# Writing out the loops inside an image in a four-layer convolution kernel

## The chip, the cores and the metric

One core of one Trainium2 chip runs the whole program. The metric is device time in microseconds, the median of several executions. The engines are TensorE (PE for its matmuls, PEld for its weight loads), VectorE (DVE), ScalarE (ACT), GpSimd (POOL) and SyncE (SP), which issues most of the DMAs.

## The reference, cut to what matters

The input is x of 4 x 32 x 256 x 256 floats (image, channel, row, column). Four layers follow each other, each with a group normalisation (16 groups) ahead and a residual around it:

```python
x = x + L0(gn(x))   # 3x3 convolution on values quantised to int8
x = x + L1(gn(x))   # DFT over rows and columns, a 32x32 channel mix at 2 x 32 x 32 modes, inverse DFT
x = x + L2(gn(x))   # 1x1 convolution, then a 5x5 depthwise convolution with filters pooled from its own output
x = x + L3(gn(x))   # per position: weights from maxima of 3x3 patches, relu, times the patch, mean of 9 taps
```

L0's scale needs the largest value of the whole input, so all of x is read once ahead of the images.

## The kernel before, in words

**Layout.** An image lies in on-chip memory as 128 partitions, one for each of 32 channels and each parity of row and column, with 128 x 128 pixels in the free dimension, padded to 130 x 130 (`img`). A tile is 4 rows of 128 pixels, 512 columns; there are `NT` = 32 tiles in an image, 16 pairs of tiles (`NPAIR`), and 16 blocks of 8 rows (`NBLK`).

**Order.** Every engine has its own program, written by hand, and they meet through counting semaphores: an instruction waits until a semaphore has reached a value. The loop over the four images is a Python loop in every engine's program, so it is written out. Inside an image some loops are Python loops too, and others are hardware loops (`Fori`): their body is stored once and runs with the loop variable in a register. In such a body a wait's value, as `b * (9 * NT) + j * 36 + (m + 13)`, and an address, as `ds(e * CR + ...)`, are worked out by register instructions of the engine's sequencer. SyncE's program has no such loop.

**Stages of an image**, with the lines that the change touches:

- Convolution L0: TensorE loops over 8 groups of 4 tiles (line 411, matmuls of line 420, nine a tile, each with a register address). ScalarE and VectorE feed and drain it, written out.
- L1: transposes (line 432, written out) that ScalarE (loop of line 625, copy of line 628) and VectorE (loop of line 1065, copy of line 1068) copy out; DFT matmuls (lines 446, 462); the mode mixing, in which GpSimd (loop of line 855, product of line 859) and VectorE (loop of line 1083, product of line 1088, sum of line 1092) work through 16 pieces of weights that SyncE loads; inverse DFT (lines 469, 481, 491); VectorE adds the result to the image and sums windows for L2 (loop of line 1127, lines 1117 and 1122).
- L2: TensorE (loop of line 504, matmuls of line 518, 36 for each block of 8 rows), GpSimd (loop of line 876, line 869), ScalarE (loop of line 701) and VectorE (loop of line 1240).
- L3's maxima: transposes (line 529), maxima on VectorE (loop of line 1259, line 1262).
- L3: the last and longest stage, described next.

**The last stage** goes through 32 tiles in pairs; two pairs are one pass of a loop on TensorE (line 575), ScalarE (line 806), GpSimd (line 880) and VectorE (line 1326). Some first or last passes are written out today: TensorE's first, VectorE's first and last, and half of ScalarE's last (`step(NT // 4 - 1, 0)`, line 809). For a tile TensorE forms nine products of five matmuls each (`product`, line 549), so 90 matmuls a pair. VectorE takes each product out of PSUM, with relu and times the patch (line 1298), into one of six buffers `pd_t`; it adds two of them up itself at three places of a pair (lines 1303 and 1307), and GpSimd adds the others one by one into the tile's sum `acc_t` (line 895; 15 adds a pair, each waiting for the one before). ScalarE prepares features of the next pair: copies into PSUM (`shifted`, lines 737 and 738), after which VectorE takes maxima (`front`, lines 1271, 1274) and subtracts (1277), and ScalarE casts (745) and copies sides (757 to 765). Between these, in ScalarE's own order, stand `restore` (line 770) and `store`:

```python
def store(j, v):
    act.wait_ge(s_acc, b * NADDS + j * (2 * ADDS) + (v // 2 * ADDS + pool_adds(v % 2, 8) + 8))
    act.dma_start(out[b, :, ds(j * (4 * TILE) + v * TILE, TILE)], acc_t[v % 4]).then_inc(s_out[v % 4], 16)
```

The store waits for GpSimd's last add of its tile, and whatever follows it in ScalarE's program, the next pair's `shifted` among it, is queued behind it. VectorE's program of a pair (`pair`, line 1279) puts `front`'s first step after its fifth product (m == 4), so its sixth waits for ScalarE's copies; TensorE may be 6 products ahead of VectorE (wait of line 560). GpSimd's fourth add in a pair's second tile waits for VectorE's sum of line 1303 (wait of line 891). SyncE loads each pair's rows from DRAM one to two pairs ahead (lines 337 to 346).

Of the kernel before, what the change touches and what calls it, by code (L numbers as in the profile page):

```python
# [82 lines left out]
def build(nc, x, w0, b0, w2, w2t, b2, mixw, w3a, w3b, bn, cst, out):  # L83
    with ExitStack() as ctx:
# [304 lines left out]
        def _(pe):  # L389
# [19 lines left out]
            for b in range(B):  # L409

                with pe.Fori(0, NCH) as e:
                    for v in range(4):
                        if v == 0:
                            pe.wait_ge(s_q, b * (NCH + 1) + e + 1)
                        if v == 3:
                            pe.wait_ge(s_q, b * (NCH + 1) + e + 2)

                        pe.wait_ge(s_t0, b * NT + e * 4 + (v + 1))
                        for s in range(9):
                            mm = T.matmul(bank(v), taps0[:, P * s:P * s + P],  # L420
                                          qgrid[:, ds(e * CR + (v * RT + s // 3), RT), s % 3:s % 3 + WO],
                                          start=(s == 0), stop=(s == 8))
                        mm.then_inc(s_conv0, 1)
# [79 lines left out]

                with pe.Fori(0, NBLK // 2) as j:
                    for p in range(2):
# [67 lines left out]
                for v in range(1, 4):  # L573
                    tile(0, v)
                with pe.Fori(1, NT // 4) as j:
                    for v in range(4):
                        tile(j, v)
# [3 lines left out]
        def _(act):  # L581
# [21 lines left out]
            for b in range(B):  # L603
# [20 lines left out]

                with act.Fori(0, NT // 4) as j:
                    for k in range(2):
                        act.wait_ge(s_l1pe, b * L1PE + j * 4 + (2 * k + 1))
                        A.copy(xt.rearrange("p (m r) -> p m r", r=HO)[:, :, ds(j * (4 * RT) + 2 * RT * k, RT)],
                               psum[:, 2 + 2 * k, :].rearrange("p (r m) -> p m r", r=RT)).then_inc(s_l1act, 1)
# [70 lines left out]
                copy_third(0, 1)  # L700
                with act.Fori(1, NBLK // 2 - 1) as j:
                    high2(j, 1)
                    sums(j - 1, 1)
                    copy_third(j, 0)
                    high2(j + 1, 0)
                    sums(j, 0)
                    copy_third(j, 1)
# [97 lines left out]

                with act.Fori(0, NT // 4 - 1) as j:
                    step(j, 0)
# [5 lines left out]
        def _(pool):  # L813
# [38 lines left out]
            for b in range(B):  # L852

                hold(pool, s_spec, b + 1)
                with pool.Fori(0, 2) as j:
                    for k in range(8):
# [18 lines left out]
                hold(pool, s_x2, b * NT + NT)  # L875
                with pool.Fori(1, NBLK // 2) as j:
                    for p in range(2):
                        transform(j, p)

                with pool.Fori(0, NT // 4) as j:  # L880
                    for v in range(4):
# [21 lines left out]
        def _(v):  # L903
# [93 lines left out]
            for b in range(B):  # L997
# [66 lines left out]

                with v.Fori(0, NT // 4) as j:
                    for k in range(2):
# [15 lines left out]
                hold(v, s_spec, b + 1)  # L1082
                with v.Fori(0, 2) as j:
                    pooled = [k for k in range(8) if k not in WR_DVE]
# [40 lines left out]
                for k in range(8):  # L1125
                    add_wave(0, k)
                with v.Fori(1, NT // 8) as j:
                    for k in range(8):
# [110 lines left out]
                add_conv2(0, 1)  # L1239
                with v.Fori(1, NBLK // 2 - 1) as j:  # L1240
                    low2(j, 1)
# [16 lines left out]
                mx_rq = mxt.rearrange("p (q r) -> p r q", q=4)  # L1258
                with v.Fori(0, NT // 4) as j:
                    for k in range(4):  # L1260
# [64 lines left out]
                pair(0, 1)  # L1325
                with v.Fori(1, NPAIR // 2 - 1) as j:
                    pair(j, 0)
# [105 lines left out]
```

## Time and profile before

| what | value |
|---|---|
| median of 3 executions | 3294.06 us (3288.66 to 3294.98) |
| the profiled execution | 3293.31 us |
| its span, first to last instruction | 3291.5 us |
| mean granted TensorE clock | 0.935 of full speed |
| instructions in the span | 45789 |
| TensorE busy | 2702.1 us (82%) |
| VectorE busy | 2660.9 us (81%) |
| GpSimd busy | 1831.8 us (56%) |
| ScalarE busy | 1813.8 us (55%) |

Register, branch and semaphore instructions, and those that issue a DMA, are counted as instructions but not as busy time. The busy shares are over the whole span; a stage can have another limit than the span's busiest engine. The profile's chain of work is followed back from the last instruction, at each step to what released it; "issue" in it is time in which the engine waited for nothing that the profile shows, and an engine's name with a q (ACTq, POOLq) is its sequencer: a register instruction, a wait, a branch or the issue of a DMA.

### The profile page before, as it was taken

The numbers are of one execution on the slowest core, as the hardware profiler recorded it, in microseconds if no ns is written. First come the engines' busy times: TensorE is split into PE (matmuls) and PEld (weight loads), VectorE is DVE, ScalarE is ACT, GpSimd is POOL, SyncE is SP. The second block draws the span as 40 slices with busy tenths as digits, with TensorE's granted clock in tenths as the row PEclk, the third lists the DMA queues.
The fourth block names the chain that finished last, engine by engine and source line by source line (L and its number), as shares of the span: only waits on it lengthen the run. The fifth ranks groups of instructions, "written<-read, shape, count | busy, mean of one in ns | idle before, by whom it ended". The sixth has DMA issues, their size and how long they took to land. (4 is left out here: it accounts for less than half of the span.)

```text
span 3291.5 us, 45789 instructions
## 1 busy us (share of the span) xinstructions
PE 2702.1 (82%) x12733; PEld 2092.2 (64%) x12733; DVE 2660.9 (81%) x3579; ACT 1813.8 (55%) x2343; POOL 1831.8 (56%) x1296
## 2 busy tenths in 40 slices
PE   0086698899989579799999569889998957979998
PEld 0035577677757458577774468667775745857776
DVE  8985887788885898688888598878888499868887
ACT  7743655566543455565655265566564345555654
POOL 2013173599950436199990317269995044629998
PEclk9998899999999789899999879999999978989999
DMA  6732001988860200688880200289885020068984
GB/s 254 251 91 77 1 0 38 231 220 222 193 174 1 77 1 0 169 222 218 209 228 32 77 0 0 56 230 225 218 192 158 1 77 0 0 183 218 227 208 114
DMA packets 116200, 419.22 MB, mean 127 GB/s; under 512 B 16565, under 2 KB 30693, under 8 KB 105354
## 3 DMA queue, kind: packets, MB, share of 16 engines
q1 hardware_dynamic: 96058, 374.65, 44.1%
q10 hardware_dynamic: 18432, 38.54, 3.3%
q0 software_dynamic: 1616, 4.90, 0.5%
q8 instruction: 44, 0.72, 0.1%
q14 instruction: 50, 0.41, 0.0%
HBM read 340.57 MB, written 75.26 MB: 126 GB/s over the span
## 5 line engine op out<-in xcount | busy, mean ns | idle before, releaser
L895 POOL TENSOR_TENSOR work<-work 128x512 f32<-128x512 f32 x960 | 1283.3, 1342 | 415.4 <-DVE work L1307 314.8
L549 PE MATMUL psum<-workr,w 128*128 128x512 f32 (+1 forms) x5760 | 1366.9, 397 | 67.2 <-ACT workr L765 50.6
L549 PEld LDWEIGHTS psum<-workr,w 128*128 128x128 f32 (+1 forms) x5760 | 1086.5, 189 | 346.9 <-issue 51.4
L1298 DVE SCALAR_TENSOR_TENSOR work<-psum,work 128x512 f32<-128x512 f32 x1152 | 738.1, 679 | 34.9 <-POOL work L895 21.4
L518 PE MATMUL psum<-workr 128*128 128x512 f32 x2304 | 553.7, 403 | 21.5 <-DVE workr L1195 21.5
L869 POOL TENSOR_TENSOR work<-img 128x520 f32 (+1 forms) x256 | 387.2, 1544 | 284.7 <-DVE workr L1167 255.7
L518 PEld LDWEIGHTS psum<-workr 128*128 128x128 f32 x2304 | 441.6, 192 | 135.0 <-issue 24.7
L859 POOL TENSOR_TENSOR work<-work 128x1024 f32<-128x1024 f32 x40 | 114.1, 2886 | 485.2 <-DVE work L1081 483.0
L745 ACT CAST workr<-psum 128x650 fp32r<-128x650 f32 x128 | 90.0, 703 | 419.4 <-DVE psum L1274 411.8
L420 PE MATMUL psum<-work,taps 128*128 x1152 | 261.6, 391 | 44.4 <-DVE work L1039 44.4
L1271 DVE TENSOR_TENSOR psum<-psum,work 128x650 f32<-128x650 f32 x128 | 107.9, 843 | 210.0 <-ACT psum L738 209.7
L420 PEld LDWEIGHTS psum<-work,taps 128*128 128x128 bf16 x1152 | 114.2, 99 | 191.2 <-issue 59.7
L668 ACT ACTIVATE workr<-work 128x1040 fp32r<-128x1040 f32 x128 | 136.5, 1073 | 76.9 <-PE psum L518 76.8
L620 ACT ACTIVATE work<-psum,small 128x512 f32<-128x512 f32 x128 | 99.3, 776 | 120.2 <-PE psum L420 94.3
L757 ACT CAST workr<-workr 32x512 fp32r<-32x512 f32 x256 | 158.8, 620 | 7.2
L758 ACT CAST workr<-workr 32x512 fp32r<-32x512 f32 x256 | 158.2, 618 | 6.2
L684 ACT ACTIVATE work<-img 128x1024 f32 (+1 forms) x64 | 68.0, 1063 | 161.5 <-DVE img L1233 161.5
L1307 DVE TENSOR_TENSOR work<-work 128x512 f32<-128x512 f32 x128 | 150.3, 1174 | 0.0
L1216 DVE SCALAR_TENSOR_TENSOR work<-psum,small,work 128x512 f32<-128x512 f32 x128 | 90.2, 747 | 57.2 <-ACT work L676 57.1
L737 ACT COPY psum<-work 64x650 f32<-64x650 f32 x128 | 89.5, 699 | 85.1 <-POOL work L895 61.0
L491 PE MATMUL psum<-consts,work 128*128 128x128 f32 x1024 | 123.8, 278 | 13.7 <-DVE img L1117 7.0
L642 ACT COPY work<-psum 64x512 f32<-64x512 f32 x64 | 57.9, 1060 | 139.9 <-PE psum L481 139.9
(188 smaller groups left out, 3582.6 us busy)
## 6 DMA issues: line engine op xcount, KB each, us to landing
work<-gn_dram SPq DMA_DIRECT2D x256, 585.0 KB, 10.7
work<-gn_dram SPq DMA_DIRECT2D x256, 146.2 KB, 3.8
work<-gn_dram SPq DMA_DIRECT2D x128, 292.5 KB, 4.8
work<-in_x SPq DMA_DIRECT2D x16, 2048.0 KB, 7.2
img<-in_x SPq DMA_DIRECT2D x32, 1024.0 KB, 11.4
work<-in_mixw SPq DMA_DIRECT2D x64, 512.0 KB, 4.9
out_x<-work ACTq DMA_DIRECT2D x120, 256.0 KB, 6.4
gn_dram<-img SPq DMA_DIRECT2D x24, 1040.0 KB, 16.9
```

What stands on the lines that cost most here:

```text
L420: mm = T.matmul(bank(v), taps0[:, P * s:P * s + P], qgrid[:, ds(e * CR + (v * RT + s // 3), RT), s % 3:s % 3 + WO], start=(s == 0), stop=( ...
L491: mm = T.matmul(bank(2 + g % 4)[:, P * r:P * r + P], gsp[:, RT * g + r, :], cs("idftw"), start=True, stop=True)
L518: mm = T.matmul(bank(banks[p]), wt[:, at:at + P], urow(part, i)[:, :, dx:dx + WO], start=(dx + n == 0), stop=(dx + n == 4))
L549: mm = T.matmul(bank(m % 6), w5[wt][0:kr, P * n:P * n + P], ft[0:kr], start=(i == 0), stop=(i == 4))
L668: A.activation(uh[p][:, half], ut[p][:, half], ACT.Identity, scale=(0.5 if h == 0 else 1.0)).then_inc(s_uh, 1)
L757: A.copy(tile4(dst[0:32, :]), left).then_inc(s_shh, 1)
L758: A.copy(tile4(dst[32:64, :]), up).then_inc(s_shh, 1)
L859: G.tensor_tensor(wr[k], wr[k], spec, ALU.mult).then_inc(s_prod, 1)
L869: G.tensor_tensor(urow(ut[p], i), x0, x1, op).then_inc(s_u, 1)
L895: G.tensor_tensor(acc_t[v], acc_t[v], pd_t[(9 * v + n) % 6], ALU.add).then_inc(s_acc, 1)
L1298: V.scalar_tensor_tensor(out=tile4(pd_t[m % 6]), in0=tile4(psum[:, m % 6, :]), scalar=0.0, in1=rv[:, q, y0:y0 + RT, x0:x0 + WO], op0=ALU.m ...
L1307: V.tensor_tensor(two, pd_t[(9 * k) % 6], two, ALU.add).then_inc(s_two, 1)
```

## The change

All fifteen hardware loops become Python loops over the same ranges; nothing else is edited. Bodies, order, buffers and semaphores stay; every wait value and address is then a constant in the instruction. The diff, cut to its lines:

```diff
-                with pe.Fori(0, NCH) as e:
+                for e in range(0, NCH):
...
-                with pe.Fori(0, NBLK // 2) as j:
+                for j in range(0, NBLK // 2):
...
-                with pe.Fori(1, NT // 4) as j:
+                for j in range(1, NT // 4):
...
-                with act.Fori(0, NT // 4) as j:
+                for j in range(0, NT // 4):
...
-                with act.Fori(1, NBLK // 2 - 1) as j:
+                for j in range(1, NBLK // 2 - 1):
...
-                with act.Fori(0, NT // 4 - 1) as j:
+                for j in range(0, NT // 4 - 1):
...
-                with pool.Fori(0, 2) as j:
+                for j in range(0, 2):
...
-                with pool.Fori(1, NBLK // 2) as j:
+                for j in range(1, NBLK // 2):
...
-                with pool.Fori(0, NT // 4) as j:
+                for j in range(0, NT // 4):
...
-                with v.Fori(0, NT // 4) as j:
+                for j in range(0, NT // 4):
...
-                with v.Fori(0, 2) as j:
+                for j in range(0, 2):
...
-                with v.Fori(1, NT // 8) as j:
+                for j in range(1, NT // 8):
...
-                with v.Fori(1, NBLK // 2 - 1) as j:
+                for j in range(1, NBLK // 2 - 1):
...
-                with v.Fori(0, NT // 4) as j:
+                for j in range(0, NT // 4):
...
-                with v.Fori(1, NPAIR // 2 - 1) as j:
+                for j in range(1, NPAIR // 2 - 1):
```

## Rows read from the trace of the kernel before

**Rows 1.** The page: span, and busy time, share and instructions of two engines.

```profile
span 3291.5 us, 45789 instructions
...
PE 2702.1 (82%) x12733; PEld 2092.2 (64%) x12733; DVE 2660.9 (81%) x3579; ACT 1813.8 (55%) x2343; POOL 1831.8 (56%) x1296
```

**Rows 2.** Stages of image 2: length, busy PE PEld DVE ACT POOL, clock, DMA.

```profile
1191.70:1330.30 138.60, 138.47 (x576) 110.44 (x576) 116.62 (x120) 71.19 (x104) 85.45 (x54) 0.98 0.00 0
...
1375.30:1721.20 345.90, 341.66 (x1440) 271.62 (x1440) 290.66 (x425) 205.36 (x310) 310.74 (x234) 0.99 0.88 218
```

**Rows 3.** TensorE's timeline, last stage: start, length, line, count, idle before.

```profile
1432.75 42.59 PE L549 MATMUL psum<-workr,w 128*128 128x512 f32 x180 [0.61 <-DVE work L1298]
1475.96 42.58 PE L549 MATMUL psum<-workr,w 128*128 128x512 f32 x180 [0.62 <-DVE work L1298]
```

**Rows 4.** Busy time of line 549 alone: PE, PEld, clock, DMA, early stage.

```profile
1379.00:1431.50 52.50, 52.50 (x226) 42.23 (x225) 1.00 0.90 212
```

**Rows 5.** Chain that ended last, two pairs of image 4: start, length, what.

```profile
3053.91 9.62 PE psum L549 x40
...
3063.56 0.96 DVE work L1303
...
3064.68 0.08 POOL work L895
...
3070.15 1.64 POOL work L895
...
3072.31 0.04 ACTq L806
...
3072.69 0.04 ACTq L735
...
3072.77 0.07 ACT psum L737
...
3075.71 9.62 PE psum L549 x40
...
3085.36 0.76 DVE work L1303
...
3091.75 1.64 POOL work L895
...
3094.17 0.08 ACT psum L737
...
3097.12 0.97 PE psum L549 x3
```

**Rows 6.** ScalarE's timeline: the store in the written-out end of image 2.

```profile
1709.68 0.35 ACTq L775 DMA_DIRECT2D out_x<-work  x1
```

**Rows 7.** GpSimd's timeline, last stage: one pair's adds.

```profile
1637.70 20.91 POOL L895 TENSOR_TENSOR work<-work 128x512 f32<-128x512 f32 x15 [0.71 <-DVE work L1303]
```

**Rows 8.** VectorE's timeline around the start of the mode mixing.

```profile
1076.80 1.04 DVE L1079 TENSOR_TENSOR work<-psum,work 128x512 f32<-128x512 f32 x1 [2.37 <-PE psum L462]
1077.87 0.19 DVE L1081 TENSOR_TENSOR work<-work 128x32 f32<-128x32 f32 x1
1078.39 1.23 DVE L1088 TENSOR_TENSOR work<-work 128x1024 f32<-128x1024 f32 x1 [0.33 <-DVE work L1081]
1079.77 1.22 DVE L1092 TENSOR_REDUCE work<-work 128x1024 f32 x1 [0.16 <-DVE work L1088]
```

**Rows 9.** Line 420 alone at full clock (as rows 4); timeline of line 446.

```profile
970.00:1018.00 48.00, 48.00 (x223) 21.43 (x222) 1.00 0.00 0
...
1818.16 28.77 PE L446 MATMUL psum<-consts,work 128*128 128x64 f32 x256 [0.98 <-DVE work L1068]
```

**Rows 10.** DMA view: instruction queues, and a small load with median us to landing.

```profile
q8 instruction: 44, 0.72, 0.1%
q14 instruction: 50, 0.41, 0.0%
...
work<-gn_dram SPq DMA_DIRECT2D x256, 146.2 KB, 3.8
```

## The prediction

> **What bounds the kernel now.** I read the page first: TensorE is busy for 82% of the span and GpSimd for 56% [rows 1], but these are averages over stages with different limits. A table by stage for the second image, which is one of four alike and 778 us long, gives each its limit [rows 2]. The last stage (line 549) takes 345.9 of the 778 us, with TensorE busy for 341.7, GpSimd for 310.7 and the DMA engines at 88%. The convolution of line 518 takes 138.6 us and TensorE is busy for 138.5: registers can cost nothing there unless they slow the matmuls themselves.
>
> So I looked at TensorE's timeline in the last stage [rows 3]. It runs 180 matmuls in one piece of 42.6 us, idles 0.61 or 0.62 us for VectorE's line 1298, and does so again: the period is 1475.96 - 1432.75 = 43.21 us. An undisturbed stretch gives the floor [rows 4]: 226 matmuls touched in 52.50 us, the two outer ones cut, so 52.5/225 = 0.2333 us each and 180 x 0.2333 = 42.0 us. TensorE thus loses 1.2 us in every 180 matmuls (two "pairs" of output tiles; 90 each, floor 21.0 us).
>
> The chain of waits says who takes it [rows 5]. It is a ring that goes round once per pair: TensorE's eight products (9.62 us), VectorE's add of line 1303, five GpSimd adds of line 895, then ScalarE, which can start the next pair's copies (lines 737, 738) only after it has issued the store of line 775, which waits for the last of those adds; then VectorE, and TensorE's twelfth product. In this execution the ring takes 3075.71 - 3053.91 = 21.80 us where ScalarE turns its loop around (pair A) and 3097.12 - 3075.71 = 21.41 us where it doesn't (pair B). Together 43.21 us, as in image 2; both are above TensorE's 21.0.
>
> **What the change does, part by part.** It writes out fifteen loops on four engines: three on TensorE, ScalarE and GpSimd each, six on VectorE. SyncE's program has no such loop and stays as it is, so no load is queued differently. Removed are register arithmetic ahead of waits and addresses, and branches. The waits stay, with constants; where an instruction has two, one becomes a wait instruction of its own (the parts written out today show this form).
>
> *ScalarE in the ring.* From the end of GpSimd's add to the start of line 737 takes, in pair A, from 3070.15 + 1.64 = 3071.79 to 3072.77, 0.98 us; in pair B from 3091.75 + 1.64 = 3093.39 to 3094.17, 0.78 us [rows 5]. In between lie two register instructions, the store's issue (a DMA instruction), in A the branch of line 806 (3072.31 to 3072.69), and register work for the waits of lines 734 and 735. The written-out form of the store stands at an image's end: its issue takes 0.35 us [rows 6]. With hops of up to 0.04 us, as between lines 735 and 737 in the chain (3072.73 to 3072.77), I make the new path 0.03 + 0.35 + 0.04 + 0.02 + 0.04 = 0.48 us. A saves 0.50, B 0.30.
>
> The branch in it costs 3072.69 - 3072.31 = 0.38 us with its register work [rows 5]. The Trainium skill (Advanced Engine Details and Errata, Control Flow Timing) puts a compare-and-branch at about 108 ns. By that figure A would save about 0.23 instead of 0.50, and the stage's gain would be 28 x 0.27 = 7.6 us smaller; the chain row has the branch in place, so the sum goes by the row.
>
> *GpSimd in the ring.* From VectorE's end (3063.56 + 0.96 = 3064.52) to the add's start (3064.68) it takes 0.16 us, with two register instructions in it. A wait instruction and the add must stay; I take 0.06 us saved, bounds 0 and 0.12 (nothing left but the 0.04 us hops). Between adds nothing but the previous add's end is waited for, and the next one's register instructions run in that time: nothing saved, bounds -0.02 to 0.02 us each.
>
> *VectorE and TensorE in the ring.* VectorE's register instructions run under its own 0.7 us operations, TensorE's under matmuls: nothing. Their cover, the queue ahead of a busy engine, stays.
>
> Sum for the stage: A saves 0.50 + 0.06 = 0.56 of the 0.80 us that it lies above TensorE's floor, B 0.30 + 0.06 = 0.36 of 0.41. What is late next is TensorE's own pace, 0.24 and 0.05 us behind. Together 0.92 us, seven times an image (the first of the eight double passes starts with nothing late), four images: 28 x 0.92 = 25.8 us. GpSimd comes close behind as the next limit: its 15 adds of a pair take 20.91 us and then it idles 0.71 us [rows 7]; 20.91 + 0.10 = 21.0 us, level with TensorE.
>
> *The mode mixing (lines 1083 to 1092).* VectorE works nearly without a pause here. Where one of its operations waits for the one before through a register, the idle time is 0.16 us; with a constant it is 1077.87 - (1076.80 + 1.04) = 0.03 us [rows 8]. Six such places an image, one of them hidden under a wait for GpSimd: 5 x 0.11 = 0.5 us, four images 2.0 us (bounds 0 and 0.7 an image).
>
> *Loop entries* on VectorE (lines 1065, 1083, 1127, 1259): entering that of line 1083 left 0.33 us idle, 0.3 more than a wait with a constant [rows 8]. The other three follow other work and wait for TensorE anyway, so I count one: 0.3 us an image, 1.2 us in all (bounds 0 and 2).
>
> *First convolution (line 420).* Every matmul has a register address there. At full clock they come at 48.00/222 = 0.216 us [rows 9], while 512 columns at 2.4 GHz take 0.213. I take 0; the bound is 288 x 0.003 = 0.9 us an image. The other TensorE loops have constant addresses.
>
> *Instruction supply.* Written-out code is fetched once and longer. Today the two instruction queues bring 44 + 50 packets [rows 10]. 12733 matmuls run, 3183 an image [rows 1], of which by the code some 1346 belong to written-out text or the first pass of a loop, so packets should grow about 3183/1346 = 2.4 times, some 130 more. The written-out line 446 ran 256 matmuls in 28.77 us, 0.112 us each, without a gap [rows 9], faster than any loop would use up text, and line 549's first 180 matmuls, written out, ran at the same 0.2333 us as the loop. I take 0; what it costs if the cover fails is a rival.
>
> Total: 25.8 + 2.0 + 1.2 = 29.0 us. The profiled execution took 3293.31 us (span 3291.5), 0.75 us under the median, so 3264.3 us by it and **3265.1 us** against the median of 3294.06.
>
> **The rivals.**
> *Only part of the ring gets shorter* (0.14). The register work runs ahead of the event it waits for, and the branch's time is mostly that of the wait behind it. Then A saves some 0.2 and B 0.1 us: 28 x 0.3 = 8.4 us, with 1.6 us elsewhere 3284. For it: on VectorE the same instructions cost nothing. Against: in the chain each stands after the add's end.
>
> *TensorE's floor is reached everywhere* (0.14). Then 1.21 us per two pairs go, 28 x 1.21 = 34 us, with 3 us from mixing and entries 3257. It needs 0.24 us more in pair A and 0.05 in B than I count; for it speaks that the first pairs, where nothing is late yet, run at the floor, so a slack once there is used up slowly.
>
> *The place goes to GpSimd* (0.06). The last of the five adds takes 1.64 us, the four before it (3070.15 - 3064.68)/4 = 1.37 us with the hop to the next [rows 5]; perhaps it meets a VectorE operation. If in the new phase two of the five do, some 0.3 us come back per pair, and if line 1303 takes pair A's 0.96 us in B too (0.76 now), 0.20 per two: 56 x 0.3 + 28 x 0.20 = 22 us, leaving 7: 3287.5 us and above, within 0.2%.
>
> *Instruction supply stalls, slower* (0.06). The place is ScalarE, VectorE and GpSimd in the last stage, whose text grows most and whose fetches share DMA engines that are 88% busy [rows 2]. The nearest price is a small load there, 3.8 us from issue to landing [rows 10]. Some 130 more packets; if 20 of them fall on the ring uncovered, 20 x 3.8 = 76 us less 29: 3341 us. It decides from 29/3.8 = 8 uncovered fetches. Against it: the first, written-out pairs of that stage show no such hole.
>
> The Trainium skill (Runtime: NRT & Kernel Launch, Instruction fetch mechanics) says that the sequencer fetches ahead in order and that crossing a block is mostly hidden, but that the buffer has only two blocks on most engines. The first half agrees with line 446; whether two blocks suffice under loaded DMA no trace here shows.
>
> That the change does nothing is excluded: the register instructions are part of the span's 45789 [rows 1] and must go.
>
> **How the numbers follow.** The forecast has 0.60. Low end: all of TensorE's idle time (34), 0.7 x 4 for mixing, 2 for entries, 1 of line 420's 3.6: 40 us, 3254. High end: the partial case, 3284, which leaves out the GpSimd and fetch cases (0.12) and some of the edge. About 0.2% (6.6 us) is what a measurement of this kernel tells from no change. Faster by more: 0.60 + 0.14 + 0.14 = 0.88; within: 0.06; slower: 0.06.
>
> **What would show it.** The page should count several thousand instructions fewer; TensorE's timeline in the last stage should have its period fall from 43.2 to 42.3 us with one gap left per two pairs; the chain should go from line 895 to line 737 in about 0.5 us; VectorE's gaps in the mixing should be 0.03 us; lines 518 and 420 should stand. GpSimd's idle time per pair should fall from 0.71 to some 0.2 us. Gaps ended by nothing that the profile shows, with an instruction packet just before their end, would make it wrong, and so would a period of 43 us with the register instructions gone.

## The result, and the profile after

The changed kernel takes **3326.39 us** (median of 5 runs, 3323.82 to 3327.32) against 3290.32 us for the kernel before in the same comparison (5 runs, 3288.46 to 3294.98): ratio 1.0105, 95% interval 1.0091 to 1.0119. It is 36 us slower where 3265.1 us were forecast; the range ended at 3284.

The page of the changed kernel, its span and busy times, and the two instruction queues:

```profile
span 3324.6 us, 37611 instructions
...
PE 2699.3 (81%) x12733; PEld 2091.0 (63%) x12733; DVE 2634.0 (79%) x3579; ACT 1813.4 (55%) x2343; POOL 1865.4 (56%) x1296
...
q8 instruction: 101, 1.65, 0.2%
q14 instruction: 91, 0.75, 0.1%
```

There are 8178 instructions fewer than in [rows 1] (register work and branches gone, some wait instructions new), and the span is 33.1 us longer. The same two stages as in [rows 2], image 2 of the changed kernel (length, busy PE, PEld, DVE, ACT, POOL, clock, DMA):

```profile
1198.80:1336.40 137.60, 136.99 (x576) 109.39 (x576) 120.70 (x121) 70.81 (x104) 87.88 (x54) 0.99 0.00 1
1380.00:1736.30 356.30, 342.32 (x1440) 272.06 (x1440) 279.95 (x424) 206.50 (x312) 315.19 (x233) 0.99 0.86 213
```

These windows are not cut alike at both ends. From the first matmul to the end of the last, the convolution is 1.5 us shorter (138.47 and 136.99 us, TensorE busy throughout), and the last stage 9.5 us longer (345.9 and 355.3 us). Counted from the first image's first matmul, between the first matmuls of successive stages, the last stage with what follows it grows from 1427.5 to 1470.8 us in four images (+43.3), and everything else shrinks from 1687.4 to 1677.8 us (-9.7); together +33.6, where the span shows +33.1. So the question is one stage.

TensorE's timeline there, changed kernel (to be held against [rows 3]):

```profile
1439.84 21.30 PE L549 MATMUL psum<-workr,w 128*128 128x512 f32 x90 [0.99 <-DVE work L1298]
1462.13 8.24 PE L549 MATMUL psum<-workr,w 128*128 128x512 f32 x34 [0.98 <-DVE work L1298]
```

One pair now takes 1462.13 - 1439.84 = 22.29 us instead of 43.21/2 = 21.6; TensorE idles about 1 us in each pair for line 1298. And VectorE's line 1298 waits for GpSimd. Its group on the page, before and then after, after the bar its idle time and who ended it:

```profile
L1298 DVE SCALAR_TENSOR_TENSOR work<-psum,work 128x512 f32<-128x512 f32 x1152 | 738.1, 679 | 34.9 <-POOL work L895 21.4
```

```profile
L1298 DVE SCALAR_TENSOR_TENSOR work<-psum,work 128x512 f32<-128x512 f32 x1152 | 750.1, 683 | 115.8 <-POOL work L895 95.1
```

The chain that ended last, changed kernel, image 4 (start, length, what), is now almost nothing but GpSimd's adds:

```profile
3088.92 0.03 issue
3088.94 0.02 POOLq L894
3088.96 0.09 issue
3089.05 1.82 POOL work L895
3090.87 0.03 issue
3090.90 0.02 POOLq L894
3090.92 0.09 issue
3091.01 1.30 POOL work L895
...
3092.44 1.31 POOL work L895
```

Two things are to be seen. Between two adds stand a wait instruction on GpSimd's sequencer (line 894, the wait for the add before) and 0.09 us until the next add starts: from one add's end to the next one's start it is 3091.01 - 3090.87 = 0.14 us. In the kernel before it was 0.08 (15 adds of about 1.29 us, two of them 1.63, in 20.91 us [rows 7]; the starts and ends in the trace give 0.078 us, against 0.143 after). From one add's start to the next one's it is 3092.44 - 3091.01 = 1.43 us, against 1.37 in [rows 5]. And one add a pair takes 1.82 us. GpSimd's timeline shows 45 adds, three pairs, with no idle time reported:

```profile
1469.04 66.65 POOL L895 TENSOR_TENSOR work<-work 128x512 f32<-128x512 f32 x45
```

(66.65 + 0.14)/3 = 22.26 us per pair: GpSimd is the bound, and the 0.71 us of [rows 7] are gone. Per pair: 13 hops of 0.143 instead of 12 of 0.078, +0.92; the idle time, -0.71; the long add, +0.46 on the sum of the fifteen. Together +0.67 us, and 64 pairs make 43 us.

**Where the hop comes from.** Every add but the first of a tile has two waits: first the operand from VectorE (line 893), then the add before (line 894). Which instruction carries which is on record in both traces. With the loop, a register instruction carries the first wait and the add itself the second. Written out, the add carries the first wait, and the second is an instruction of its own ahead of it. Our reading of the longer hop is that an add that carries the wait for its predecessor is ready to start when that one ends, while an add behind a separate wait instruction still has its 0.09 us to go. No row shows this inside of the hop by itself; e1 below shows that the order of the two waits sets the price.

### The profile page after: what moved, and what is told of

The parts are those of the page before. It is cut to its first block and busy times, and to the rows that moved or that the text cites. A ratio compares the mean times of both kernels' runs of the same rounds, so it can differ in the third digit from the quotient of the medians.

```text
span 3324.6 us, 37611 instructions
## 1 busy us (share of the span) xinstructions
PE 2699.3 (81%) x12733; PEld 2091.0 (63%) x12733; DVE 2634.0 (79%) x3579; ACT 1813.4 (55%) x2343; POOL 1865.4 (56%) x1296
## 5 line engine op out<-in xcount | busy, mean ns | idle before, releaser
L895 POOL TENSOR_TENSOR work<-work 128x512 f32<-128x512 f32 x960 | 1306.1, 1366 | 436.4 <-DVE work L1307 317.1
L1298 DVE SCALAR_TENSOR_TENSOR work<-psum,work 128x512 f32<-128x512 f32 x1152 | 750.1, 683 | 115.8 <-POOL work L895 95.1
L869 POOL TENSOR_TENSOR work<-img 128x520 f32<-128x520 f32 x256 | 398.2, 1587 | 267.7 <-DVE workr L1167 238.6
L420 PE MATMUL psum<-work,taps 128*128 128x512 bf16 x1152 | 259.8, 389 | 47.9 <-DVE work L1039 47.9
L684 ACT ACTIVATE work<-img 128x1024 f32<-128x1024 f32 x64 | 68.0, 1063 | 175.8 <-DVE img L1233 175.8
L1219 DVE TENSOR_TENSOR img<-img,work 128x1024 f32<-128x1024 f32 x64 | 134.0, 2094 | 2.2
L491 PEld LDWEIGHTS psum<-consts,work 128*128 128x128 f32 x1024 | 117.0, 192 | 20.7 <-DVE img L1117 13.6
```

The costliest lines, as they stand in the source:

```text
L420: mm = T.matmul(bank(v), taps0[:, P * s:P * s + P], qgrid[:, ds(e * CR + (v * RT + s // 3), RT), s % 3:s % 3 + WO], start=(s == 0), stop=( ...
L491: mm = T.matmul(bank(2 + g % 4)[:, P * r:P * r + P], gsp[:, RT * g + r, :], cs("idftw"), start=True, stop=True)
L869: G.tensor_tensor(urow(ut[p], i), x0, x1, op).then_inc(s_u, 1)
L895: G.tensor_tensor(acc_t[v], acc_t[v], pd_t[(9 * v + n) % 6], ALU.add).then_inc(s_acc, 1)
L1219: V.tensor_tensor(split, split, mid.rearrange("p (two t w) -> p two t w", two=2, w=WO), ALU.add).then_inc(s_x3, 1)
L1298: V.scalar_tensor_tensor(out=tile4(pd_t[m % 6]), in0=tile4(psum[:, m % 6, :]), scalar=0.0, in1=rv[:, q, y0:y0 + RT, x0:x0 + WO], op0=ALU.m ...
```

## The experiments

All times are medians against the kernel before on the same chip in the same comparison (3290 to 3294 us); "pair" is the period of the last stage.

| kernel | us | ratio (95%) | pair, us |
|---|---|---|---|
| changed kernel | 3326.4 | 1.0105 (1.0091 to 1.0119) | 22.26 |
| e1, two waits swapped | 3285.7 | 0.9979 (0.9970 to 0.9988) | 21.60 |
| e2, GpSimd's loop back | 3284.3 | 0.9979 (0.9970 to 0.9988) | 21.6 |
| e3, only GpSimd's loop written out | 3325.4 | 1.0106 (1.0091 to 1.0122) | 22.15 |
| e4, e1 with ScalarE's loop back | 3283.3 | 0.9972 (0.9962 to 0.9982) | 21.6 |
| e5, e1 without VectorE's sums | 3236.0 | 0.9827 (0.9812 to 0.9842) | 21.0 |
| e6, e1, one add moved to VectorE | 3279.3 | 0.9953 (0.9940 to 0.9967) | 21.65 |
| e7, the same add moved in the kernel before | 3309.2 | 1.0047 (1.0033 to 1.0061) | 22.07 |
| e8, e6 with ScalarE's loop back | 3300.2 | 1.0018 (1.0009 to 1.0027) | 21.97 |
| e9, e6 and the store moved | 3243.7 | 0.9848 (0.9834 to 0.9861) | 21.0 |
| e10, e9 with ScalarE's loop back | 3243.4 | 0.9849 (0.9835 to 0.9862) | 21.0 |
| e11, both moves in the kernel before | 3251.1 | 0.9904 (0.9873 to 0.9935) | 21.0 |
| e12, only the store moved, kernel before | 3269.6 | 0.9928 (0.9915 to 0.9941) | 21.32 |
| e13, e1 and the store moved | 3267.3 | 0.9924 (0.9910 to 0.9937) | 21.35 |
| e14, changed kernel and the store moved | 3309.3 | 1.0053 (1.0039 to 1.0067) | 21.94 |

### The hop between GpSimd's adds: e1, e2, e3

e1 is the changed kernel with the wait for the previous add written ahead of the other one:

```diff
                             else:
+                                pool.wait_ge(s_acc, ... pool_adds(k, n) + 7)
                                 if k == 1 and n == 4:
                                     pool.wait_ge(s_two, ...)
                                 else:
                                     pool.wait_ge(s_pd, ...)
-                                pool.wait_ge(s_acc, ... pool_adds(k, n) + 7)
```

> The changed kernel with one edit: for GpSimd's adds of line 895 the wait for its own previous add (s_acc) stands ahead of the wait for VectorE's product (s_pd), instead of behind it. Theory 1 (the wait for the previous add has become an instruction of its own that must pass before the add is issued, so that every hop between adds takes 0.143 us instead of 0.078, 13 times a pair, and GpSimd's chain of 15 adds sets the pace at 22.27 us a pair): the hops go back to about 0.08 us, the pair to about 21.1 us, the time to about 3265 us, below the kernel before. Theory 2 (supply of instructions: the text is as long as in the changed kernel): the time stays at 3326 us. Theory 3 (adds that meet VectorE operations in a new phase are the cause, the hops only fill what is free): the hops shrink, but the time stays above 3310 us.

e2 puts GpSimd's loop of line 880 back into the changed kernel; e3 writes out that loop alone in the kernel before.

> The changed kernel with GpSimd's loop of the last stage (line 880) alone put back; the fourteen other loops stay written out. Theory 1: hops of 0.078 us again, pair at about 21.1 us, some 3266 us. Theory 2, if it is GpSimd's own text that is short of supply: the same 3266 us; if it is the text of any other engine: 3310 us or more. Theory 3: above 3300 us.

> The kernel before with GpSimd's loop of line 880 alone written out. Theory 1: the hops of 0.143 us and a GpSimd-bound pair of about 22.3 us, as in the changed kernel, 28 x 1.3 = 36 us slower than before in the last stage and none of the other loops' gains: about 3328 to 3335 us. Theory 2, supply of the longer text of ScalarE, VectorE or TensorE: at the time of the kernel before, 3291 us.

By the whole time, e3 alone makes the loss (1.0106), e2 alone takes it away, and e1 takes it away with everything still written out, so with as much text to supply: it is the place of one wait. By stages e3 makes 35.5 of the 43.3 us: its last stage with what follows takes 1463.0 us. In a steady pair its GpSimd still idles 0.63 us and has no add of 1.81 us; that collision comes only with other loops written out too. Its total, a little under the 3328 to 3335 us expected, comes near the changed kernel's because its other stages take 1681.6 instead of 1677.8 us. But neither e1 nor e2 comes to 3265. GpSimd's timeline in e1:

```profile
1482.58 20.90 POOL L895 TENSOR_TENSOR work<-work 128x512 f32<-128x512 f32 x15 [0.69 <-DVE work L1303]
1504.18 16.59 POOL L895 TENSOR_TENSOR work<-work 128x512 f32<-128x512 f32 x12 [0.70 <-DVE work L1303]
```

The pair is 1504.18 - 1482.58 = 21.60 us, as before the change, and the idle time is back at 0.7. Of the gain forecast for the last stage nothing is there; e1's 7 us come from the other stages (its last stage with what follows takes 1428.6 us, the rest 1678.4).

### ScalarE's savings: e4

e1 with ScalarE's loop of line 806 put back, which should return the register work and the branch to the ring:

```diff
-                for j in range(0, NT // 4 - 1):
+                with act.Fori(0, NT // 4 - 1) as j:
                     step(j, 0)
                     step(j, 1)
```

> The swapped version with ScalarE's loop of the last stage (line 806) put back. It measures the term of the prediction for ScalarE. If ScalarE's register work and branch lie on the ring as the prediction has it, 0.50 + 0.30 us come back per two pairs: 28 x 0.80 = 22 us more than the swapped version alone. If they are hidden (the partial rival), less than 8 us more.

It costs nothing: 3283.3 against 3285.7 us. So the ring's savings either don't exist or are lost on the way. The timelines say which. In the kernel before, GpSimd and then VectorE around one line 1303:

```profile
1483.14 2.66 POOL L895 TENSOR_TENSOR work<-work 128x512 f32<-128x512 f32 x2
...
1486.50 1.29 POOL L895 TENSOR_TENSOR work<-work 128x512 f32<-128x512 f32 x1 [0.71 <-DVE work L1303]
...
1485.60 0.74 DVE L1303 TENSOR_TENSOR work<-work 128x512 f32<-128x512 f32 x1
```

The add under way ends at 1483.14 + 2.66 = 1485.80. Line 1303 started at 1485.60 and ends at 1486.34, 0.54 us after the add. The same place in e1:

```profile
1479.23 2.66 POOL L895 TENSOR_TENSOR work<-work 128x512 f32<-128x512 f32 x2
...
1481.06 1.37 DVE L1303 TENSOR_TENSOR work<-work 128x512 f32<-128x512 f32 x1
```

The add ends at 1481.89, line 1303 at 1482.43, again 0.54 us later. It started much earlier in its add (1481.89 - 1481.06 = 0.83 instead of 0.20 us ahead of the add's end), and took 1.37 instead of 0.74 us. In the kernel before the two kinds of pair start 0.20 and 0.49 us ahead (line 1303 then takes 0.74 and 1.04 us), in e1 both some 0.83: VectorE arrives 0.63 and 0.34 us earlier, which is what the prediction had as savings (0.56 and 0.36). In e4 it starts 0.29 and 0.49 us ahead, and the end is the same. **The savings were real, and line 1303 waited them out.** In all these rows line 1303, which reads two operands from SBUF (on-chip memory), doesn't complete until some 0.55 us after the GpSimd add that is under way. The next add needs its result, so GpSimd idles 0.54 + 0.16 = 0.70 us whatever the ring saves.

### Without the collision: e5

e1 with copies from PSUM in place of the two sums of lines 1303 and 1307, issued just ahead of the product that the sums followed. These sums are left out of what is computed.

```diff
-                            V.tensor_tensor(pd_t[13 % 6], pd_t[12 % 6], pd_t[13 % 6], ALU.add).then_inc(s_two, 1)
+                            V.tensor_copy(pd_t[13 % 6], psum[:, m % 6, :]).then_inc(s_two, 1)
...
-                            V.tensor_tensor(two, pd_t[(9 * k) % 6], two, ALU.add).then_inc(s_two, 1)
+                            V.tensor_copy(pd_t[(9 * k + 1) % 6], psum[:, m % 6, :]).then_inc(s_two, 1)
```

> The swapped version with VectorE's sums of lines 1303 and 1307 replaced by copies of the same size out of PSUM, issued just ahead of the product that they followed. It leaves out the sums of products 0 and 1 of each tile and 3 and 4 of each pair's second tile, and puts a copy of the current product in their place. Theory A (the last stage is bound by GpSimd: its adds and VectorE's sums of two tiles in on-chip memory cannot run at once, each such sum waits for the add under way and then holds GpSimd up, 0.70 us at line 1303 and 0.34 us at each line 1307): without such sums GpSimd never idles for 0.7 us and all its adds take 1.29 us, a pair needs 15 x 1.29 + 13 x 0.08 = 20.4 us on GpSimd, TensorE's 21.0 us sets the pace, and the time falls by 60 x 0.6 = 34 us against the swapped version, to about 3251 us. Theory B (the ring through ScalarE, VectorE and TensorE sets the period of 21.61 us, as in the prediction): the copies take as long as the sums alone did, and the time stays within 8 us of the swapped version's 3285.7 us.

3236.0 us, 15 us less than theory A had: TensorE has no gap in the last stage any more, and GpSimd's mean add falls from 1342 ns in the kernel before to 1294. From TensorE's timeline and e5's page:

```profile
1469.77 30.52 PE L549 MATMUL psum<-workr,w 128*128 128x512 f32 x130
```

```profile
L895 POOL TENSOR_TENSOR work<-work 128x512 f32<-128x512 f32 x960 | 1237.0, 1294 | 408.2 <-DVE work L1303 315.5
```

So without the two sums nothing is left above TensorE's floor. But e5 doesn't isolate the collision. The copies take as long on VectorE as an undisturbed sum (687 ns), yet they stand ahead of the product, so GpSimd gets its signal one VectorE operation sooner, and the ring is shorter by that too. That the collision is at work is read from the rows of line 1303 in e1 and e4, not from e5's time.

### One add fewer on GpSimd: e6, e7, e8

Line 1303 now sums two products in both tiles of a pair, so GpSimd has 14 adds instead of 15:

```diff
-ADDS = 8 + 7
-NTWO = 3 * NPAIR
+ADDS = 7 + 7
+NTWO = 4 * NPAIR
...
-                        if m == 14:
-                            v.wait_ge(s_pd, b * (9 * NT) + j * 36 + (18 * p + 32))
-                            V.tensor_tensor(pd_t[13 % 6], pd_t[12 % 6], pd_t[13 % 6], ALU.add).then_inc(s_two, 1)
+                        if n == 5:
+                            v.wait_ge(s_pd, b * (9 * NT) + j * 36 + (18 * p + 9 * k + 23))
+                            V.tensor_tensor(pd_t[(m - 1) % 6], pd_t[(m - 2) % 6], pd_t[(m - 1) % 6], ALU.add).then_inc(s_two, 1)
```

> The swapped version with one add more moved from GpSimd to VectorE: products 3 and 4 are summed on VectorE in both tiles of a pair instead of in the second alone, so that GpSimd has 14 adds a pair instead of 15. Nothing is left out. Theory A: GpSimd's pair falls from 21.61 by 1.37 and rises by 0.34 to 0.70 for the new exclusion, to 20.6 to 20.9 us; TensorE's 21.0 us becomes the pace: about 28 to 34 us less than the swapped version, 3252 to 3258 us. Theory B: VectorE has one operation more in the ring and nothing is gained: 3286 us or more.

> The same moved sum in the kernel before, with all its hardware loops. It shows what the loops cost once GpSimd is not the bound. Theory A with the prediction's ring behind it: the ring's 21.80 and 21.41 us would then be what is late, so this stays 20 us or more above the version written out. Theory A alone, registers and branches hidden everywhere in the last stage: only the 7 to 9 us between the kernel before and the swapped version remain between this and the version written out, so about 3260 to 3266 us.

> The written-out version with the moved sum, with ScalarE's loop of line 806 put back. If ScalarE's branch and register work come onto the path once GpSimd is relieved, up to 22 us more than the version without it; if they stay hidden, within 4 us of it.

e6 missed: 3279.3 us. Its timelines, GpSimd and then ScalarE:

```profile
1471.61 9.73 POOL L895 TENSOR_TENSOR work<-work 128x512 f32<-128x512 f32 x7 [1.48 <-DVE work L1303]
1482.04 9.75 POOL L895 TENSOR_TENSOR work<-work 128x512 f32<-128x512 f32 x7 [0.69 <-DVE work L1303]
1493.26 9.76 POOL L895 TENSOR_TENSOR work<-work 128x512 f32<-128x512 f32 x7 [1.47 <-DVE work L1303]
```

```profile
1489.19 0.34 ACTq L775 DMA_DIRECT2D out_x<-work  x1
1489.62 0.70 ACT L737 COPY psum<-work 64x650 f32<-64x650 f32 x1 [0.93 <-POOL work L895]
```

The pair is 1493.26 - 1471.61 = 21.65 us, and GpSimd now idles 1.48 + 0.69 us in it. Here the prediction's ring does bind: ScalarE stands 0.93 us for the add behind the store of line 775. And the loop costs what was forecast: e8 (ScalarE's loop back) is 20.9 us slower than e6. The prediction's terms for ScalarE alone were 0.50 + 0.30 = 0.80 us, 28 times: 22.4 us. The price was right, in a kernel in which the ring binds. In the kernel before, with all loops (e7), relieving GpSimd even loses 16 us. We take it that the ring is then the bound, at 22.07 us, with a second sum and its wait in it; no run tests this apart.

### The store out of the ring: e9, e10, e11, e12

The stores of tiles 1 and 3 (line 775) are issued only after the next pair's first copies:

```diff
                     if more:
                         shifted(jn, pn, 0)
+                    if not first:
+                        store(j - (p == 0), 3 if p == 0 else 1)
+                    if more:
                         high(jn, pn, 0)
...
                         side_low(jn, pn, 1)
-                    store(j, 2 * p + 1)
```

The lines of the last stage stand five further down in these kernels: their line 900 is line 895, their 1303 is 1298, their 1308 is 1303.

> The kernel with the sum moved to VectorE (e6), and every second store (line 775, of tiles 1 and 3) issued only after the next pair's first copies (lines 737, 738). Theory 1, the ring is real once GpSimd has time to spare: in e6 line 737 waits 0.93 us for GpSimd's add behind the store of line 775, once per pair; with the store behind the copies, that time and the store's own 0.34 us leave the ring, TensorE runs at its 21.0 us per pair instead of 21.64, and some 60 pairs x 0.64 = 38 us go: 3241 us (3237 to 3248). Rival, the ring closes elsewhere (VectorE's sums held by GpSimd's adds, or line 1271's order on VectorE): 21.5 us and more per pair, 3270 us and above.

> e9 with ScalarE's loop of line 806 kept as a loop (the first pass written out). Theory 1: in e9 ScalarE has about 0.9 + 0.3 - 0.6 = 0.6 us to spare per pair, which covers the branch and register work of 0.38 us and most of the rest, so that the loop costs nothing to 8 us: 3241 to 3249 us. Rival, the loop's register work lies on the path whatever the order: about 20 us as between e6 and e8, so 3261 us.

e9 and e10 came as expected. TensorE and ScalarE in e9:

```profile
1474.77 45.48 PE L549 MATMUL psum<-workr,w 128*128 128x512 f32 x194
```

```profile
1485.88 0.61 ACT L765 CAST workr<-workr 32x512 fp32r<-32x512 f32 x1
1486.52 0.70 ACT L737 COPY psum<-work 64x650 f32<-64x650 f32 x1
1486.99 0.34 ACTq L775 DMA_DIRECT2D out_x<-work  x1
```

No gap is left on TensorE, line 737 follows line 765 at once, and the store is issued beside the copy. With this slack ScalarE's loop, worth 20.9 us between e6 and e8, is worth nothing between e9 and e10.

> The kernel before, with all its loops, with only the moved sum (e7) and the moved store (e9): nothing of the writing out is in it but ScalarE's first pass. Theory 1, registers cost time only where no other engine's work covers them, and with the ring loosened the last stage covers them on every engine: the last stage runs at TensorE's 21.0 us per pair as in e9, and what is left is what the writing out saves in the other stages, 4 x 2.3 = 9 us: 3253 us (3249 to 3257). Rival, loops on VectorE, TensorE or GpSimd still lie on the path in the last stage: about 3265 us, e9 and the whole of the difference between e7 and e6, 3309 and 3279, less what ScalarE's part of it was (21 us).

> The kernel before with only the store moved behind the next pair's first copies. Theory 1, the last stage of the kernel before is bound by GpSimd's fifteen adds and the time it is held behind line 1303, not by the ring: taking 0.9 to 1.3 us per pair out of the ring changes nothing, 3293 us (3289 to 3296). Rival, the ring as the prediction had it binds: the pair falls from 21.6 towards 21.0 us and the kernel to about 3260 us.

e11 came within 2 us of what was expected: with both moves, the kernel before with its loops (but for ScalarE's first pass) takes 3251.1 us, and writing everything else out, with GpSimd's waits swapped, brings 7.4 us (e9), all outside the last stage (1684.6 against 1677.3 us). Two of e11's six runs took 3276.2 and 3277.4 us, the other four 3249.7 to 3251.7; hence its wide interval. **e12 missed.** After e1 and e4 the last stage had been taken for bound by GpSimd alone; nothing should have changed, and 22.8 us went (the rival had about 3260 us). GpSimd's timeline in e12, three pairs:

```profile
1469.74 63.88 POOL L900 TENSOR_TENSOR work<-work 128x512 f32<-128x512 f32 x45
```

(63.88 + 0.08)/3 = 21.32 us per pair, without idle time. The collision at the sum (their line 1308; GpSimd, then VectorE):

```profile
1476.80 3.00 POOL L900 TENSOR_TENSOR work<-work 128x512 f32<-128x512 f32 x2
...
1477.48 1.17 DVE L1308 TENSOR_TENSOR work<-work 128x512 f32<-128x512 f32 x1
```

The sum still waits for the add under way (which ends at 1478.09, the sum at 1478.65), but the add after it is not the one that needs the sum: it starts at once and is only stretched, to 1.63 us. So the ring is there in the kernel before as well, and what it gains counts in steps: savings vanish in line 1303's wait until it comes one add earlier, and then the idle 0.70 us shrink at once to a hop of 0.08, for one more add stretched by 0.34.

### The step: e13, e14

> The written-out kernel with GpSimd's two waits swapped (e1) and every second store moved behind the next pair's first copies; no sum moved. Theory 2, the ring is there but moves in steps: what is saved in it only makes VectorE's line 1303 start earlier inside a GpSimd add that it must wait out, until it is so early that GpSimd's next add is no longer held; e12 crossed that step and ran at 15 adds and 15 short hops, 21.32 us per pair. Then e13 does the same, 21.32 us per pair with no idle time on GpSimd, plus what the writing out saves in the other stages (9 us): 3270 - 9 = 3261 us (3257 to 3265). Rival, ring purely bound by durations: ScalarE's written-out path takes another 0.3 to 0.6 us out of it, TensorE's 21.0 us are reached: 3243 us.

> The changed kernel as it is, with only the store moved as in e12. Theory 2, with GpSimd's hops of 0.143 us its fifteen adds and hops fill the pair (22.27 us, no idle time), so that it alone binds and the ring has time to spare: nothing changes, 3326 us (3322 to 3329). Rival, the ring still binds somewhere in the changed kernel: 10 us or more are gained, as e12 gained 23.

GpSimd's timeline, three pairs each, in e13 and then in e14:

```profile
1469.11 63.97 POOL L900 TENSOR_TENSOR work<-work 128x512 f32<-128x512 f32 x45
```

```profile
1468.91 65.68 POOL L900 TENSOR_TENSOR work<-work 128x512 f32<-128x512 f32 x45
```

e13: 64.05/3 = 21.35 us per pair, the step and not TensorE's 21.0, although ScalarE's part was shorter still. The total was 6 us above what was expected, because the other stages of e12 were already 6.4 us shorter than those of the kernel before, with the same loops: their sum differs by that much between kernels that are alike there (e3 has 1681.6 us, e12 1681.0, the kernel before 1687.4), and adding the 9 us counted it twice.

e14 missed: 3309.3 instead of 3326 us. It is the 10 us or more of the rival, but not by the rival's way: GpSimd has no idle time in either kernel, as expected, but its adds don't take the same time. Its line 895 (900) in the two kernels, three pairs each (duration ns: shortest, median, longest):

```profile
L895 POOL TENSOR_TENSOR work<-work x45: 1277/1295/1807, 1469.0 to 1534.1; 128x512 f32<-128x512 f32 x45
```

```profile
L900 POOL TENSOR_TENSOR work<-work x45: 1278/1292/1558, 1468.9 to 1533.0; 128x512 f32<-128x512 f32 x45
```

In the changed kernel line 1303 starts in the gap between two adds, GpSimd starts 0.03 us later and stands still until VectorE is through:

```profile
1471.70 0.68 DVE L1303 TENSOR_TENSOR work<-work 128x512 f32<-128x512 f32 x1
```

```profile
1471.73 1.81 POOL L895 TENSOR_TENSOR work<-work 128x512 f32<-128x512 f32 x1
```

So who comes first pays nothing and the other waits: VectorE 0.68 and GpSimd 1.81 us here, 1.37 and 1.29 in e1. Moving the store moved line 1303 out of that gap; the add costs 1.55 instead of 1.81, and the pair 21.94 instead of 22.26. "GpSimd alone binds" was right, "so nothing else can matter" was not. Why in the changed kernel line 1303 settles exactly in the gap wasn't tried.

## Why the prediction was wrong, step by step

- **"The waits stay, with constants; where an instruction has two, one becomes a wait instruction of its own", and "Between adds ... nothing saved, bounds -0.02 to 0.02 us each".** This is the step that turned the sign. The form was seen and its price taken from the number of instructions, not from which of the two waits ends up in the sequencer. It was +0.065 us in each of 13 hops, 0.85 us a pair on an engine with 0.71 us of idle time. With the idle time used up and one add stretched longer, 0.67 us a pair came of it, where 0.46 us a pair (0.92 in two) were to be saved. The bounds didn't hold the value. e1, e2 and e3 show it from three sides.
- **The rival for a slower kernel** was placed in the supply of instructions. That cover held: 192 packets instead of 94 [rows 10], 98 more where some 130 were expected, and nothing in the last stage waits for them. The Trainium skill's remark (Runtime: NRT & Kernel Launch, Instruction fetch mechanics) that crossing blocks is mostly hidden agrees with e9, where TensorE runs 194 written-out matmuls without a gap beside DMA engines that are 94% busy.
- **ScalarE in the ring, A -0.50, B -0.30; GpSimd's entry -0.06.** For ScalarE right in size: line 1303 comes 0.63 and 0.34 us earlier in e1, and the loop costs 20.9 us in e8 against 22.4. GpSimd's entry, from the end of line 1303 to the add, is 1482.58 - 1482.43 = 0.15 us in e1 against 0.16 before, so hardly anything of the 0.06 is there. Wrong in worth: "What is late next is TensorE's own pace". Late next was the GpSimd add that line 1303 must wait out.
- **[rows 7]** was read as a slack that shrinks from 0.71 to 0.2. It was a fixed price: end of the add, 0.54 us for line 1303 to complete, 0.16 to the next. The sign was in [rows 5]: line 1303 took 0.96 us in pair A and 0.76 in B, and an operation of one shape whose time depends on the phase is waiting for something. The rival "the place goes to GpSimd" had the collision, from the add of 1.64 us, but priced it as a nuisance of the new phase instead of finding it in the old one. That its 3287.5 us lies near e1's 3285.7 is luck: it adds new waiting to a shorter ring, and e1's last stage has the old waiting and the old length.
- **The mode mixing, 0.5 us an image, and the loop entries, 0.3.** The gaps went as forecast, the time didn't. After the change the reduction follows the product 1092.85 - (1090.58 + 2.23) = 0.04 us after its end instead of 1085.35 - (1083.10 + 2.11) = 0.14, but the next product itself takes 0.10 us longer (the one before it 0.12). VectorE's timeline, before and then after:

```profile
1083.10 2.11 DVE L1088 TENSOR_TENSOR work<-work 128x1024 f32<-128x1024 f32 x1
1085.35 1.22 DVE L1092 TENSOR_REDUCE work<-work 128x1024 f32 x1
1086.49 2.01 DVE L1088 TENSOR_TENSOR work<-work 128x1024 f32<-128x1024 f32 x1
```

```profile
1090.58 2.23 DVE L1088 TENSOR_TENSOR work<-work 128x1024 f32<-128x1024 f32 x1
1092.85 1.22 DVE L1092 TENSOR_REDUCE work<-work 128x32 f32<-128x1024 f32 x1
1093.98 2.11 DVE L1088 TENSOR_TENSOR work<-work 128x1024 f32<-128x1024 f32 x1
```

From one product to the next it is 1086.49 - 1083.10 = 3.39 us before and 1093.98 - 1090.58 = 3.40 after. It is line 1303's story again: line 1088, 1.23 us when it starts with GpSimd idle, ends 1.08 us after the GpSimd product (line 859) that is under way, in all five such places of image 2 in both kernels. From the first product to the last reduction of the image it is 32.73 us before and 32.66 after, 0.07 us instead of 0.5. The entry of the loop idles 1085.96 - (1085.62 + 0.19) = 0.15 instead of 0.33 us [rows 8]; 0.03 was forecast:

```profile
1085.62 0.19 DVE L1081 TENSOR_TENSOR work<-work 128x32 f32<-128x32 f32 x1
1085.96 1.23 DVE L1088 TENSOR_TENSOR work<-work 128x1024 f32<-128x1024 f32 x1
```

- **Lines 420 and 518, 0.** The matmuls keep their pace (0.2171 and 0.2351 us from start to start in both kernels), so register addresses cost TensorE nothing. The stages are still up to 1.5 us shorter, and these are most of the 9.7 us against the 3.2 forecast for everything but the last stage. How much of the 9.7 is owed to writing out stays open: with the loops in place the same sum is 1687.4 us in the kernel before, but 1684.6 in e11, 1683.8 in e7, 1681.6 in e3 and 1681.0 in e12; written out it is 1675.3 to 1678.4. The first 5 us of line 518 in image 2, before and then after (PE busy, PEld busy, clock):

```profile
1191.80:1196.80 5.00, 4.99 (x12) 3.94 (x13) 0.50 0.00 0
```

```profile
1198.80:1203.80 5.00, 4.99 (x16) 4.02 (x17) 0.71 0.02 3
```

The stage opens at the lower of the clock's two levels, 1.2 GHz (0.50), and how long it stays there differs: four matmuls more in the same 5 us. The loops alone don't set it: in image 3 of the changed kernel the stage is as long as before (138.41 against 138.46 us from its first matmul to the end of its last), and in e12, with all its loops there, 0.5 us shorter in image 2. What sets it was not settled.

## What to carry to other kernels

Where an instruction needs two waits, look in the trace at which of them rides on the instruction and which stands ahead of it; here it paid to let the one that ends last ride. Writing a loop out can turn the two around without a line of the body being edited. Before costing a saving on a ring of waits, look for an operation in it whose duration depends on its phase: it takes up what is saved until the phase crosses a whole step, and a second look at the idle time next to it (the same 0.7 us in every pair) tells that it is a price and not a slack. The gaps of the mode mixing show the same on a smaller scale: a gap ahead of such an operation is no saving either. The two moves of e11, one sum from GpSimd to VectorE and one store behind two copies, are worth 41 us with the loops in place, and 50 us with them written out and the waits swapped (e9, 0.9848); alone, the first cost 16 us and the second brought 23.

## What the runs showed of the hardware

- A wait that stands ahead of an instruction on GpSimd makes the hop from one add's end to the next add 0.143 us (changed kernel, e3, e14); with the same wait on the add itself it is 0.078 (before, e1, e2). The Trainium skill (Perfetto Trace Analysis, Identifying Dependency Chains) says that instructions waiting on several engines may have a wait instruction inserted before them. The trace agrees (POOLq L894), and adds the price and that the order in the source decides which wait it is: in this program the later one.
- VectorE operations with both operands in SBUF and GpSimd's adds exclude each other. If the add is under way, the VectorE operation ends about 0.55 us after it, whenever it started (or 0.68 us after its own start, where that is later: 0.07 us ahead of the add's end in the changed kernel, it ended 0.61 after it); if VectorE is 0.03 us ahead, the add takes 1.81 instead of 1.29 us; an add that follows such a collision takes 1.55 to 1.63. Line 1298, with one operand in PSUM, took 0.67 to 0.69 us in all its 1152 instances. The Trainium skill (SBUF — State Buffer, SBUF: two separate sides) calls the port pair of the two engines an exclusive lock, taken by whichever starts first, for the whole instruction. The trace agrees on both sides, but each wait is about 0.13 us shorter than the recorded durations laid end to end would make it: 0.55 instead of 0.68 us after the add, and 1.81 us for the add instead of (0.68 - 0.03) + 1.29 = 1.94. The page doesn't say what the rows show besides: that the waiting time is booked as the operation's own duration, so that no view lists it as idle.
